# Attention inside a recurrent kernel: fp32 weights stream past the values, and the second block of heads is put ahead of the steps

## The reference, cut to what matters

```
scores = einsum('bhqd,bhkd->bhqk', qt, kt) / sqrt(16)     # 16 heads of 16 features
attn   = softmax(scores)
out_h  = expmap0(einsum('bhqk,bhkd->bhqd', attn, vt))
x = mobius_add(x, expmap0(g_msa * logmap0(plin(from_heads(out_h), w_o, b_o))))
...
x = x + block(x, cond)
a = xw_t + prev_h @ Wh                                     # 512 steps, 4 gates of 256
next_c = sigmoid(f) * prev_c + sigmoid(i) * tanh(g)
next_h = sigmoid(o) * tanh(next_c)
```

## Time and profile before

| | |
|---|---|
| median of 3 runs | 1553.42 us (1553.27 to 1554.94) |
| the profiled execution | 1551.88 us, span 1550.0 us |
| busy, share of the span | PE 91%, PEld 78%, DVE 75%, ACT 59%, POOL 30% |
| granted TensorE clock, mean | 0.946 |
| chain that ended last | PE 62%, DVE 24%, ACT 6%, issue 6% |

### The profile page before, as it was taken

How to read it: one execution, slowest core, us unless ns; L and a number is a source line. 1 busy time by engine, 2 the same in 40 slices (tenths; PEclk the granted TensorE clock), 3 DMA queues, 4 the chain that set the end, 5 groups by cost and what they waited for, 6 DMA issues and landing times.

```text
span 1550.0 us, 65350 instructions
## 1 busy us (share of the span) xinstructions
PE 1418.1 (91%) x25395; PEld 1205.5 (78%) x25395; DVE 1159.0 (75%) x6593; ACT 913.9 (59%) x3340; POOL 466.3 (30%) x1230
## 2 busy tenths in 40 slices
PE   3786854799999999999999999999999999999998
PEld 3674543688888888888888888888888888888886
DVE  5898763688887878788878787877676676766665
ACT  2687952767766676767675767574545444444433
POOL 2453120043251515151515151515131322220000
PEclk9997556799999999999999999999999999999999
DMA  8000000000000000000000000000000000000000
GB/s 267 6 1 1 1 1 1 5 3 3 10 3 10 3 10 3 10 3 10 3 10 3 10 3 10 3 10 3 10 3 9 3 10 3 6 3 6 3 7 5
DMA packets 16718, 18.48 MB, mean 12 GB/s; under 512 B 6036, under 2 KB 15384, under 8 KB 16408
## 3 DMA queue, kind: packets, MB, share of 16 engines
q1 hardware_dynamic: 13016, 10.51, 2.3%
q10 hardware_dynamic: 3392, 3.81, 1.0%
HBM read 12.21 MB, written 2.10 MB: 9 GB/s over the span
## 4 chain that ended last, share of the span: by engine, by line
PE 62%; DVE 24%; ACT 6%; issue 6%; POOL 1%; DMA 1%; DVEq 0%; ACTq 0%; POOLq 0%
PE psum L784 26%; PE psum L823 17%; PE psum L759 3%; PE psum L659 3%; PE psum L724 3%; DVE cnew L1522 2%; ACT ot L1045 2%; DVE weights L1273 2%; DVE hl L1531 2%; DVE hl L1529 2%; PE psum L731 2%; PE psum L739 2%; PE psum L774 2%; PE psum L671 2%; DVE gO L1517 1%
## 5 line engine op out<-in xcount | busy, mean ns | idle before, releaser
L784 PEld LDWEIGHTS psum<-hl,wh 128*128 128x128 f16 x16384 | 470.6, 96 | 80.7 <-DVE hl L1531 72.7
L784 PE MATMUL psum<-hl,wh 128*128 128x8 f16 x16384 | 515.4, 172 | 15.2 <-DVE hl L1531 6.2
L823 PE MATMUL psum<-zeros,ident 128*128 128x256 f16 (+2 forms) x3374 | 415.7, 263 | 7.3 <-DVE gF L1515 2.0
L823 PEld LDWEIGHTS psum<-zeros,ident 128*128 128x128 f16 x3374 | 308.0, 98 | 78.8 <-DVE gF L1515 17.2
L1039 ACT ACTIVATE tA<-gA 128x16 f32<-128x16 f32 x512 | 110.5, 216 | 427.2 <-DVE gA L1513 426.7
L1273 DVE TENSOR_TENSOR weights<-w,weights 128x256 f16<-128x256 f32 x512 | 202.7, 418 | 15.0 <-ACT weights L940 14.8
L1513 DVE TENSOR_REDUCE gA<-psum 128x16 f32<-128x32 f32 x512 | 96.3, 188 | 126.1 <-PE psum L784 118.9
L1529 DVE TENSOR_TENSOR hl<-ot 128x8 f16<-128x8 f32 x512 | 89.9, 176 | 95.1 <-ACT ot L1045 94.1
L946 ACT ACTIVATE w<-psum 128x512 f32<-128x512 f32 x256 | 154.3, 603 | 5.6 <-DVE weights L1273 4.5
L1045 ACT ACTIVATE ot<-cnew 128x8 f32<-128x8 f32 x512 | 109.7, 214 | 81.0 <-DVE cnew L1522 29.8
L940 ACT ACTIVATE weights<-psum 128x512 f16<-128x512 f32 x256 | 153.6, 600 | 3.9 <-PE psum L671 3.9
(11 more groups left out here) (299 smaller groups left out, 2207.5 us busy)
## 6 DMA issues: line engine op xcount, KB each, us to landing
arena<-in_x_dram SPq DMA_DIRECT2D x4, 512.0 KB, 9.1
wf<-in_L_cond_w_f_dram SPq DMA_DIRECT2D x2, 1024.0 KB, 20.0
xr<-in_x_dram SPq DMA_DIRECT2D x64, 32.0 KB, 1.9
out_dram<-place SPq DMA_DIRECT2D x64, 32.0 KB, 1.6
qTs<-in_L_cond_w_ada_dram ACTq DMA_DIRECT2D x1, 1536.0 KB
oT<-in_L_cond_Wh_dram ACTq DMA_DIRECT2D x1, 1024.0 KB, 12.6
wx<-in_L_cond_Wx_dram SPq DMA_DIRECT2D x1, 1024.0 KB, 16.6
rows<-in_L_cond_b_ada_dram ACTq DMA_DIRECT2D x4, 128.0 KB, 14.9
```

Source lines behind the costliest of these rows:

```text
L784: last = mm(cols, wh16[:, half, kc, (g0 + c) * P:(g0 + c + 1) * P], hl[:, :, kc, :, 2].rearrange("p e b -> p b e"), start=False, stop=c == ...
L823: mm(pF[:, D:D + n], ident16[:], zeros[:, 0:n], start=False, stop=False, skip_group_check=True)
```

## The change

The exponential is made once, in fp32, into a ring of 8 buffers. The weighted sum is turned round: the values with a column of ones (128x17, fp32) are stationary, and the fp32 weights stream past them, 4 chunks of 128 columns for a head. The result stands transposed, 17 partitions for a head, four heads on the partitions 0, 32, 64 and 96 of `pV`. When a tile's 16 heads are done, ACT copies `pV` out (`oc`), PE turns it back by 4 transposes, and DVE takes the reciprocal and copies `uo` out. ACT does `oc` three slots after the tile's last head; DVE's low halves go; POOL writes the fp32 values straight into `vs`, two operations a tile less. The diff below is cut; its last piece is DVE's. Heads ahead of the steps (`batched`) are summed four at a time, chunk by chunk, 3 slots after the fourth; a head beside the steps has two of its chunks in the second slot after its scores and two in the third. Block 1 moves to slots -82 to -19. EARLY goes; RAISE stands at t < 4 and t % 64 == 23 up to 330; `beside` counts 512 columns for two chunks.

```diff
-BESIDE, EARLY, RAISE, HEADS_END = 2640, 2900, 4500, 300
+BESIDE, RAISE, HEADS_END = 2640, 4500, 330
+BEFORE_STEPS = -82
-    return (FIRST + i, -19 + i, 46 + 2 * i, 174 + 2 * i)[block]
+    return (FIRST + i, BEFORE_STEPS + i, 46 + 2 * i, 174 + 2 * i)[block]
+def batched(n):
+    return head_slot(n // 4 * 4 + 3) < 0
...
-        vs = sb("vs", [P, B, NB, H, 2 * HD + 1], F16)
+        vs = sb("vs", [P, B, NB, H, HD + 1])
-        weights = sb("weights", [P, 4, 2, T], F16)
-        w32 = sb("w32", [P, 4, T])
+        w32 = sb("w32", [P, 8, T])
...
-            def weighted(m):
-                pe.wait_ge(s["t_l"], 2 * m + 2)
-                if m % 8 == 0 and m > 0:
-                    pe.wait_ge(s["t_u"], m // 8)
-                for kc in range(NB):
-                    for wl in range(2):
-                        last = mm(pV[:, h % 8 * W1:(h % 8 + 1) * W1], weights[:, m % 4, wl, kc * P:(kc + 1) * P], vs[:, k % B, kc, h, :], ...)
+            def weighted(first, last, chunks=range(NB)):
+                if chunks[0] == 0:
+                    pe.wait_ge(s["t_e"], last + 1)
+                    if first % H == 0 and k >= 1:
+                        pe.wait_ge(s["t_u"], k)
+                for kc in chunks:
+                    for m in range(first, last + 1):
+                        done = mm(pV[32 * (h % 4):32 * (h % 4) + HD + 1, h // 4 * P:(h // 4 + 1) * P], vs[:, k % B, kc, h, :],
+                                  w32[:, m % 8, kc * P:(kc + 1) * P], start=kc == 0, stop=kc == NB - 1, skip_group_check=True)
+            def turned_back(k):
+                pe.wait_ge(s["t_c"], k + 1)
+                for i in range(4):
+                    last = tr(pV[:, i * P:(i + 1) * P], oc[:, i * P:(i + 1) * P], ident[:])
             def attention(t):
-                if t - 5 in HEAD_AT:
-                    weighted(HEAD_AT[t - 5])
+                m = HEAD_AT.get(t - 4, 0)
+                if m % H == H - 1:
+                    turned_back(m // H)
+                if t - 3 in HEAD_AT:
+                    m = HEAD_AT[t - 3]
+                    if batched(m) and m % 4 == 3:
+                        weighted(m - 3, m)
+                for half in range(2):
+                    m = HEAD_AT.get(t - 2 - half, 0)
+                    if m > 0 and not batched(m):
+                        weighted(m, m, range(2 * half, 2 * half + 2))
                 if t in HEAD_AT:
                     scores(HEAD_AT[t])
-                wanted = RAISE if t < 4 or t % 64 in (0, 1) and t < HEADS_END else BESIDE if t >= 2 * RING else EARLY
+                wanted = RAISE if t < 4 or t % 64 == 23 and t < HEADS_END else BESIDE
...
             def attention(t):
+                m = HEAD_AT.get(t - 4, 0)
+                if m % H == H - 1:
+                    v.wait_ge(s["t_T"], k + 1)
+                    d.reciprocal(num("rd", 2 * H)[:, k % 2 * H:(k % 2 + 1) * H], two[:, :, HD]).then_inc(s["t_rd"], 1)
+                    d.tensor_copy(uo[:, k % 2, :].rearrange("p (h e) -> p h e", e=HD), two[:, :, 0:HD]).then_inc(s["t_u"], 1)
```

More of the change, by code:

```diff
@@ L403, in values @@
                 ch.link(g.tensor_scalar(num("fv", H), num("f", 48)[:, 2 * H:3 * H], V_UP, None, ALU.mult))
[L404 to L405 removed]
+                g.tensor_tensor(vs[:, k % B, k // B, :, 0:HD], lin_of(k)[:, 2, :].rearrange("p (h e) -> p h e", e=HD),
                                 num("fv", H).unsqueeze(2).to_broadcast([P, H, HD]), ALU.mult).then_inc(s["p_v"], 1)
[L407 to L410, removed]
             for turn in range(-1, NT + 1):
@@ L661, in scores @@
                 last.then_inc(s["t_S"], 1)
-            def weighted(m):
-                k, h = m // H, m % H
-                pe.wait_ge(s["t_l"], 2 * m + 2)
-                if m % 8 == 0 and m > 0:
-                    pe.wait_ge(s["t_u"], m // 8)
-                for kc in range(NB):
-                    for wl in range(2):
-                        last = mm(pV[:, h % 8 * W1:(h % 8 + 1) * W1], weights[:, m % 4, wl, kc * P:(kc + 1) * P], vs[:, k % B, kc, h, :],
-                                  start=kc == 0 and wl == 0, stop=kc == NB - 1 and wl == 1, skip_group_check=True)
-                last.then_inc(s["t_AV"], 1)
-            def attention(t):
-                if t - 5 in HEAD_AT:
-                    weighted(HEAD_AT[t - 5])
+            def weighted(first, last, chunks=range(NB)):
+                k = first // H
+                if chunks[0] == 0:
[4 more added lines that the diff above has]
+                    for m in range(first, last + 1):
+                        h = m % H
+                        done = mm(pV[32 * (h % 4):32 * (h % 4) + HD + 1, h // 4 * P:(h // 4 + 1) * P], vs[:, k % B, kc, h, :],
+                                  w32[:, m % 8, kc * P:(kc + 1) * P], start=kc == 0, stop=kc == NB - 1, skip_group_check=True)
+                if chunks[-1] == NB - 1:
+                    done.then_inc(s["t_AV"], last + 1 - first)
+            def turned_back(k):
+                pe.wait_ge(s["t_c"], k + 1)
+                for i in range(4):
+                    last = tr(pV[:, i * P:(i + 1) * P], oc[:, i * P:(i + 1) * P], ident[:])
+                last.then_inc(s["t_T"], 1)
+            def attention(t):
+                m = HEAD_AT.get(t - 4, 0)
[9 more added lines that the diff above has]
+                        weighted(m, m, range(2 * half, 2 * half + 2))
                 if t in HEAD_AT:
@@ L934, in attention @@
             def attention(t):
[L936 to L940, removed]
+                m = HEAD_AT.get(t - 3, 0)
+                if m % H == H - 1:
+                    act.wait_ge(s["t_AV"], m + 1)
+                    if m // H >= 1:
+                        act.wait_ge(s["t_T"], m // H)
+                    A(oc, pV, ACT.Copy).then_inc(s["t_c"], 1)
                 if t in HEAD_AT:
@@ L1267, in _ @@
                                        ALU.mult, ALU.subtract).then_inc(s["w_lo"], 1)
[L1269 to L1273, removed]
             def attention(t):
[L1277 to L1283, removed]
+                m = HEAD_AT.get(t - 4, 0)
+                if m % H == H - 1:
+                    k = m // H
+                    v.wait_ge(s["t_T"], k + 1)
                     if k >= 2:
@@ L1286, in attention @@
                         v.wait_ge(s["m_sq"], k - 1)
[L1287 to L1291, removed]
+                    two = pV.rearrange("p (h e) -> p h e", e=2 * HD)
+                    d.reciprocal(num("rd", 2 * H)[:, k % 2 * H:(k % 2 + 1) * H], two[:, :, HD]).then_inc(s["t_rd"], 1)
+                    d.tensor_copy(uo[:, k % 2, :].rearrange("p (h e) -> p h e", e=HD), two[:, :, 0:HD]).then_inc(s["t_u"], 1)
             asked = 4
```

28 lines of the change are left out of this document (11 added, 17 removed).

## The result

The changed kernel takes 1607.61 us (median of four runs, 1601.07 to 1610.25) against 1554.09 for the kernel before beside it: ratio 1.0338, 95% interval 1.0303 to 1.0373. The profiled execution took 1605.15 us, its span 1603.4, 53.4 more than the span before.

A forecast was written before the change was run, and what follows sets the result against it. PE, nearly always occupied, was taken to end the slots beside the steps, so added PE work lengthens them beyond the slack. -17.8 + 51 - 17 = +16 us on 1551.9: 1568, or 1570 in the runs' terms; own range 1556 to 1590, outer 1540 to 1630.

The forecast's parts named there:

- step 70: An even step with a head's scores: two chunks in, two products of zeros out, 2.7 us gates to gates.
- the take-out: Slot where DVE copies a finished tile out and PE's next chunk waits: 4.4 us instead of 2.7, seven times.
- steps 0 to 47: First 48 steps, left without heads: 2.33 us each plus 4.0 for raised slots, -17.8 us from 133.7.
- the batch of four heads: 32 records on PE ahead of the steps, column groups running at once: 1.07 us at 2.4 GHz.
- Steps 48 to 303: The 256 steps with heads beside them: +51 us, from 76.5 of PE time, -26.3 slack, -7.6, +12.0, -3.2.
- the new wait: Between tiles of blocks 2 and 3, PE's next chunk waits for DVE's copy: +12.0 us over seven times.
- Ahead of the steps: Heads and rows work before the first step: -17 us, from -19, +3, +10 and -11.
- The first 64 heads: First stretch ahead of the steps: 16 rounds of 2.85 us plus 4 x 1.2, 50 us for 69.3, -19.
- the rival on the clock: Ahead of the steps: 1.2 GHz stays, four heads take 4.2 us, 1613; chance 0.23 shared with column groups one after another.
- The 45 heads beside the rows work: Block 1's later heads, in slots that took 43.5 us before: half hidden, +10 us, bounds 0 and +22.
- The faster rival: Block 1's heads cost nothing ahead of the steps: sum there -42 us, time 1545; chance 0.13.
- The cheap sum: Beside the steps the sum costs less, say one record in place of two: time near 1520; chance 0.04.

The follow-up runs named there:

- no_wait: Changed kernel, but beside the steps a tile's first head has all four chunks one slot later, so none waits for DVE's copy: 1583.41 us, ratio 1.019.
- before_wait: Kernel before with one wait added: in seven slots PE waits behind its gate products for the end of DVE's step: 1586.90 us, ratio 1.0217.
- before_moved: Kernel before with only block 1's heads moved ahead, to slots -82 to -19, sums still fp16 pairs, EARLY kept: 1572.44 us, ratio 1.0117.
- pool_copies: Changed kernel with POOL's two operations a tile put back in the set-up, into a tile nobody reads: 1614.81 us, ratio 1.0379.
- four512: Changed kernel, beside the steps four heads share a chunk's time, one chunk every second slot, none waiting for the tile's copy: 1523.03 us, ratio 0.979.
- four1024: The kernel of four512 with eight records of four heads counted as 1024 columns in place of 512, so fewer zeros: 1545.96 us, ratio 0.9948.

## Why the prediction was right in its sign and short in its size

The bound was read rightly: PE ends the slots beside the steps, and what is added there lengthens them. Right in size were step 70 (2.71 for 2.7), the take-out (4.43 for 4.4), steps 0 to 47 (-18.1 for -17.8) and the batch of four heads (1.07 us for 1.07). So were the 1.2 us for each tile ahead, which name no row: at full clock the four rounds of a tile take 12.76 us, 1.2 more than four of 2.89. The bounds ahead of the steps don't add up: the terms as bounded give -34 to +6, not -45 to +5; the forecast doesn't rest on them.

**Steps 48 to 303, +77.2 for +51.** This is the term that was mis-sized, by the price of the new wait above all. The forecast carried the level of before, "all at 2.4 GHz", over to steps that it had itself given an idle PE. The new wait was priced at its own length, +12.0, and seven steps of 4.43 us in place of 2.61 are 12.7; the clock's 17 us were missing. no_wait shows that they hang on the wait (15.3 us went with it beside its own 11.6), before_wait that a wait alone brings them. Of the other 9.2 us, 0.7 are these, and 6.5 are slack counted as used up and not used: of the 26.3 us of waiting for the state, 6.5 are still there. The last 2 us I can't place; the 7.6 us for DVE's low halves were never measured by themselves.

**Ahead of the steps, -17 forecast, -6.0 measured, by two errors of opposite sign.** From the first scores on 142 us were forecast and 163.2 came. The first 64 heads took 58.6 for 50: the clock stood at 0.50 until 168.1, and a round of four heads, from batch to batch, took 4.15 us there, as the rival had worked out (4.2), and 2.89 after it:

```profile
143.29 1.91 PE L668 MATMUL psum<-w,vs 128*17 128x128 f32 x32
...
147.44 1.91 PE L668 MATMUL psum<-w,vs 128*17 128x128 f32 x32
...
179.53 1.07 PE L668 MATMUL psum<-w,vs 128*17 128x128 f32 x32
...
182.42 1.07 PE L668 MATMUL psum<-w,vs 128*17 128x128 f32 x32
```

In the 32.5 us of half clock fit 7.8 rounds, at 1.25 us more each 9.8 us. So the rival on the clock held for part of the stretch. The 45 heads beside the rows work took 60.8 for 53.5: "I let half hide" was too kind, since a fifth hid, here as in before_moved with the old sums. The last part took 28.8 for 24. Against these 21 us the set-up, as pool_copies shows, gave 10.0: "POOL's two copies a tile fall in the set-up ... and bring nothing" was wrong, because it asked what waits for POOL and not whom POOL slows. That the sum ahead is off by 11 us and not by 21 is luck.

The faster rival, heads of block 1 for nothing, is refuted by the same rows. The cheap sum is refuted too: a pair of chunks takes 0.55 us.

## What to carry to other kernels

Where PE is kept at 2.4 GHz by work that nobody needs, price a new wait, and any zeros taken away, twice: by its length and by the steps that may follow at 1.2 GHz. Narrow stationary operands were cheap here where four column groups were taken in turn, beside the steps as well as in the stretch where a batch is easy (four512). Of an engine's hidden work ask also which other engine's operations it lengthens.

## What the runs showed of the hardware that was not expected

A single idle time of 1.48 us on PE, with fp16 gate products ahead of it and fp16 scores and zeros behind it, came with the half clock. Without any idle time over 0.55 us, 512 columns fewer in every second slot gave 72 us of it. The Trainium skill (TensorE: Matmul & The Clock Gate, Part 1: The HAM clock gate) ties the low level to an idle PE; before_wait agrees in that the low level came with PE's idle times, 82 us with seven of them. But four1024 and the kernel before, with 9.1 and 8.1 us of idle time in pieces, differ by 72 us of half clock, so the sum of idle time alone doesn't say when. Four narrow products of four column groups taken in turn started 5 to 8 ns apart. A DVE operation beside POOL's copies took 658 ns for 426.
